# First loads, statistics and skip terms of a gated long-convolution layer in another order

## The reference, cut to what matters

```python
def _layernorm(x, axis=-1, eps=1e-05):
    m = jnp.mean(x, axis=axis, keepdims=True)
    v = jnp.var(x, axis=axis, keepdims=True)
    return (x - m) / jnp.sqrt(v + eps)

def _L0_xattn_ref(k, v, q, ssm_kernel, D, head_dim):      # head_dim 8, 16 heads, L = 256
    kv = jnp.einsum('bhil,bhjl->bijhl', k_, v_)
    kv_f = jnp.fft.rfft(kv, n=fft_size)
    kernel_f = jnp.fft.rfft(ssm_kernel, n=fft_size)
    y = jnp.fft.irfft(kv_f * kernel_f, n=fft_size)[..., :L]
    out = y + kv * D[None, None, None, :, None]           # the skip term
    out = jnp.einsum('bijhl,bhil->bjhl', out, q_)
...
x = x + jnp.tanh(g_xattn[0]) * _L0_xattn_ref(ctx_2048, ctx_2048, _layernorm(x, axis=-1), L0_xattn_ssm_kernel, L0_xattn_D, 8)
```

## Time and profile before

| what | value |
|---|---|
| runs of the kernel | median 958.02 us (956.0 to 959.27, 3 runs) |
| the profiled execution, its own time | 956.07 us |
| its span in the trace | 953.6 us |
| PE busy, share of the span | 910.1 us, 95% |
| DVE, ACT, POOL busy | 605.7, 545.4, 200.7 us |
| mean granted TensorE clock | 0.99 |

### The profile page before, as it was taken

How to read it: one execution, slowest core, us unless ns; L and a number is a source line. 1 busy time by engine, 2 the same in 40 slices (tenths; PEclk the granted TensorE clock), 3 DMA queues, 4 the chain that set the end, 5 groups by cost and what they waited for, 6 DMA issues and landing times.

```text
span 953.6 us, 13986 instructions
## 1 busy us (share of the span) xinstructions
PE 910.1 (95%) x4744; PEld 723.5 (76%) x4744; DVE 605.7 (64%) x1396; ACT 545.4 (57%) x947; POOL 200.7 (21%) x171
## 2 busy tenths in 40 slices
PE   5799889999999999979999988999999999999998
PEld 5799758877788888846666666778788888888886
DVE  6678654555564565478888765656955466556554
ACT  3222043433444335458889675777777777777775
POOL 5899400000000001137777530000000000000000
PEclk9899999999999999999999998999999999999999
DMA  8100120323211351024554305444444344444443
GB/s 299 62 1 1 34 84 17 107 80 114 94 51 35 96 187 58 32 88 156 176 169 156 121 7 166 133 133 132 133 146 150 98 133 133 147 149 136 139 129 109
DMA packets 58101, 104.62 MB, mean 110 GB/s; under 512 B 7312, under 2 KB 13840, under 8 KB 57648
## 3 DMA queue, kind: packets, MB, share of 16 engines
q1 hardware_dynamic: 57312, 103.60, 34.0%
q10 hardware_dynamic: 720, 0.14, 0.1%
HBM read 101.29 MB, written 2.42 MB: 109 GB/s over the span
## 4 chain that ended last, share of the span: by engine, by line
PE 49%; DVE 3%; ACT 2%; issue 1%; DMA 1%; POOL 0%; DVEq 0%; SPq 0%; ACTq 0%; POOLq 0%
PE bank L1111 19%; PE bank L1078 18%; PE bank L1370 3%; PE bank L1381 2%; PE bank L1363 1%; PE bank L1362 1%; PE bank L1358 1%; PE bank L1390 1%; PE bank L534 1%; PE bank L770 1%; DVE X L668 0%; DMA Gf<-gates 0%; DVE shifted_scores L1560 0%; PE bank L752 0%; DVE max L1554 0%
## 5 line engine op out<-in xcount | busy, mean ns | idle before, releaser
L1078 PE MATMUL bank<-xhf,whif 128*128 128x512 f32 x528 | 212.0, 401 | 1.5 <-ACT rf L848 1.5
L1078 PE MATMUL bank<-xlf,whif 128*128 128x512 f32 x528 | 208.2, 394 | 0.0
L1078 PE MATMUL bank<-xhf,wlof 128*128 128x512 f32 x528 | 208.1, 394 | 0.0
L867 ACT ACTIVATE yhif<-yf 128x512 fp32r<-128x512 f32 x200 | 124.1, 622 | 86.6 <-DVE yf L952 82.5
L966 DVE TENSOR_TENSOR yf<-yf,Gf 128x512 f32<-128x512 f32 x125 | 86.5, 692 | 129.3 <-ACT yf L856 122.1
L1111 PE MATMUL bank<-yhif,whif 128*128 128x512 f32 x400 | 159.5, 399 | 7.0 <-DVE ylof L731 6.5
L1111 PE MATMUL bank<-yhif,wlof 128*128 128x512 f32 x400 | 157.9, 395 | 0.0
L1111 PE MATMUL bank<-ylof,whif 128*128 128x512 f32 x400 | 156.9, 392 | 0.0
L731 DVE TENSOR_TENSOR ylof<-yf,yhif 128x512 fp32r<-128x512 f32 x196 | 134.4, 687 | 30.0 <-ACT yhif L867 29.7
L850 ACT ACTIVATE rf<-bank 128x512 f32<-128x512 f32 x136 | 81.0, 596 | 80.7 <-PE bank L1078 80.6
L1078 PEld LDWEIGHTS bank<-xhf,whif 128*128 128x128 f32 x528 | 99.3, 188 | 24.5 <-ACT rf L848 1.9
(11 more groups left out here) (135 smaller groups left out, 1212.2 us busy)
## 6 DMA issues: line engine op xcount, KB each, us to landing
Gf<-gates SPq DMA_DIRECT2D x157, 256.0 KB, 3.7
wrawf<-in_wu SPq DMA_DIRECT2D x68, 256.0 KB, 2.6
k_blocks_sb<-in_k_blk SPq DMA_DIRECT2D x64, 256.0 KB, 4.1
wrawf<-in_wu SPq DMA_DIRECT2D x32, 384.0 KB, 3.2
v_slot<-in_v_rows SPq DMA_DIRECT2D x16, 256.0 KB, 2.7
ctx_windows<-in_ctx_win SPq DMA_DIRECT2D x3, 1024.0 KB, 11.7
toeplitz<-in_kpad SPq DMA_DIRECT2D x4, 512.0 KB, 9.2
X<-in_x SPq DMA_DIRECT2D x4, 512.0 KB, 9.3
```

What stands on the lines that cost most here:

```text
L867: act.activation(yhi[:, K % S, :], y[:, K % S, :], ACT.Copy).then_inc(s_yh, 1)
L1078: last = pe.matmul(o, w_[:, Nu % S, wc], x_[:, c, xs], start=(m == 0), stop=(m == 5))
```

## The change

It moves calls; no instruction is added or taken out.

- SP: the first 512 KB of x (`rows(0)`) are loaded before the first windows and the first kernel table.
- POOL: `pairs(1)` comes behind the first `deviations` and `shifts`.
- ACT: the small loads go in the order `dbc`, `anti`, `ident`; `normed(0)` comes ahead of the second `squares` and of the tanh of the gates.
- PE: the two `turn` calls of group 0 come behind step 1 instead of step 2.
- DVE: the first statistics come ahead of all tables; `table(0)` and `table(1)` follow; `table(2)` comes behind the weighing of step 0 and `table(3)` behind that of step 2. The wait for the tanh moves to group 1.

```diff
@@ SP
+                    rows(0)
                     window_quad(0)
                     kernel_table(0)
-                    rows(0)
                     for hq in range(1, 4):
@@ POOL
                     pairs(0)
-                    pairs(1)
                     pool.wait_ge(s_mh, 1)
                     deviations(pool, "a", 0)
                     shifts(pool, "a", 0)
+                    pairs(1)
                     pairs(2)
@@ ACT
+                    act.dma_start(dbc[:], d_skip.partition_broadcast(P)).then_inc(s_ca, 16)
+                    act.dma_start(anti[:], anti_c).then_inc(s_ca, 16)
                     act.dma_start(ident[:], ident_c).then_inc(s_c, 16)
-                    act.dma_start(anti[:], anti_c).then_inc(s_ca, 16)
-                    act.dma_start(dbc[:], d_skip.partition_broadcast(P)).then_inc(s_ca, 16)
...
                     squares(0)
+                    normed(0)
+                    squares(1)
                     act.wait_ge(s_tl, 32)
                     act.activation(tg[:], graw[:], ACT.Tanh).then_inc(s_tg, 1)
-                    squares(1)
-                    normed(0)
@@ PE
-                            if g == 0 and r == 2:
+                            if g == 0 and r == 1:
                                 for half in range(2):
                                     turn(0, half)
@@ DVE
-                    dve.wait_ge(s_ca, 32)
-                    table(0)
                     input_moments(0)
                     dve.wait_ge(s_st, st.n)
                     variances(dve, "a", 0)
                     negated(dve, "a", 0)
-                    for hq in range(1, 4):
+                    dve.wait_ge(s_ca, 32)
+                    for hq in range(2):
                         table(hq)
-                    dve.wait_ge(s_tg, 1)
                     for g in range(NG):
                         for r in range(8):
                             weigh(g, r // 2, r % 2)
+                            if g == 0 and r in (0, 2):
+                                table(2 + r // 2)
                             if g == 0 and r < 3:
                                 input_moments(r + 1)
...
+                            if g == 1 and r == 0:
+                                dve.wait_ge(s_tg, 1)
```

## The result

| kernel | runs | median us | range |
|---|---|---|---|
| before | 16 | 957.42 | 953.6 to 960.13 |
| changed | 16 | 961.1 | 959.91 to 965.35 |

The ratio of changed to before is 1.005, with a 95% interval of 1.0036 to 1.0063: slower by 3.4 to 6.0 us, 4.8 at the middle; the two medians differ by 3.7. The predicted median was 961.1 us, in a range of 957.5 to 963.5. The profiled execution took 960.74 us, its span is 958.3 us, 4.7 us more than before.

The account below looks back on a forecast made before the run. Stage a was taken as bound by PE's queue from 37.15 us, begun by DVE's statistics chain. Weighing 2.2 us earlier and two tables 1.1 + 4.2 later gave +3.1: median 958.02 + 3.1 = 961.1 us, range 957.5 to 963.5.

Parts of the forecast that it names:

- What bounds the stage: Stage a: from 37.15 us PE's queue, whose end moves one for one with the start of that stretch.
- ident third, and the start of weighing: ACT's queue, PE, DVE: ident lands at 7.3, step 0 starts at 12.5, weighing at 18.7, 2.2 us earlier.
- early-start rival: ident lands by 6.3, weighing starts by 17.7, moments(3) only 1.2 us late, median 959.2 us; chance 0.25.
- signs of being wrong: L405 of 0.34 us beside L255; window group well before 23.6; or weighing starting after 20.9.
- Step 0: PE: starts at 12.5 us instead of 9.03, behind the filler that waits for ident.
- the power: POOL's L139 of 12 columns, for groups 1 to 3: near 35.5 us.
- The hold of table(3): DVE: table(3), due at 27.2, held by POOL's instructions until 31.5; 4.2 us later in the chain.
- L255 holds DVE: Assumed like L246 and L248; the rival without hold: table(3) takes 1.14 us, median 958.0; chance 0.10.
- table(2): DVE: falls at about 20.3 into POOL's pause and is free, adding 1.1 us to the chain.
- hold of the first variances: Group 0's variances, 1.62 us beside pairs(1), no longer stand beside it; costed at 0, covered by steps 0 and 1.
- POOL's pattern: Window group kept landing at 23.64 us; POOL then works without a pause until 31.35.
- clock's price at the turn: PE at granted 0.50 after its gap: same 1.7 us price; rival of a longer clock, 962.8 us, chance 0.15.

Follow-up runs that it names:

- a1: The changed kernel with all four tables back ahead of the first weighing; ratio to before 1.0012.
- c4: c3 with table(3) behind weigh(0), where POOL idles, and the power for groups 2 and 3 two steps later on POOL; ratio to before 0.9951.
- c2: The kernel before with table(3) behind the variances of groups 1 to 3, all else as before; ratio to before 1.0005.
- a2: The changed kernel with ACT's small loads in the old order (ident, anti, dbc); ratio to before 1.0043.
- c5: c4 with filler matmuls in PE's gap ahead of the last four sums; ratio to before 0.9926, median 950.91 us.
- b1: The kernel before with the tables moved alone: table(2) behind weigh(0), table(3) behind weigh(2); ratio to before 1.0031.
- c3: c2 with the statistics of group 1 by themselves, ahead of the first weighing; ratio to before 0.9985.
- a5: The changed kernel with table(3) behind the variances of groups 1 to 3; ratio to before 1.0042, in a second run 1.004.
- a4: The changed kernel with POOL's pairs(5) behind the power and shift of groups 1 to 3; ratio to before 1.0054.

## Why the prediction was right, and where it wasn't

*What bounds the stage.* Right. The `turn` of group 1 was late by 4.51 us, PE behind it was busy throughout, and the span grew by 4.7. a1 and c4 confirm it from both sides. That the end moves one for one with the `turn` holds within about 1 us: c2 lost its 1.0 us at the turn again. The prediction has no term for the clock in the last sums, which cost 1.6 to 3.0 us in seven of the thirteen executions. It was luck that the changed kernel's profiled execution wasn't one of them.

*ident third, and the start of weighing.* This step failed. I took a landing at 7.3, a filler of 5.15 us and a first weighing at 18.7, 2.2 us earlier than before. Measured were 9.15, 6.28 (to 15.43) and 21.48, 0.55 later. The landing varied, 7.0 to 9.5 us over six executions with that order; from the filler's start to step 0 it was 5.2 to 6.6 us over all the executions but a2's, where step 0 waited for the first table, with the granted clock rising sooner or later in it. I had one value for each and no spread. The landing that I had taken it from, `dbc` third in the old order, varied as well: 5.7 us from its issue in the kernel before and 5.5 in c5, but 7.1 to 7.5 in b1, c2, c3 and c4. With 7.4, the forecast would have been near the 9.15 that came. The early-start rival fell with it: `ident` landed by 6.3 us in none of the seven executions in which it was third.

For that rival I had read the Trainium skill, "DMA: Bandwidth & Descriptors", section "Queues, rings and completion order", as if taking the queue rows in turn kept ACT's small loads from being late. The runs contradict that reading and not the rule itself: with the same loads on SP's queue `ident` took 2.9 us from issue to landing in the first place of ACT's queue (a2) and 5.3 to 7.7 in the third, so what made it late stood in its own queue.

With it came true one of the signs of being wrong that I had named, weighing that starts after 20.9. Step 0 (15.43 for 12.5), the power (36.87 for 35.5) and the `turn` were each later than forecast.

*The hold of table(3).* Right in mechanism, off in place and size. I had it due at 27.2, with 4.2 us to the next instruction; it came at 29.89 and took 2.91, of which 1.86 are the hold. Since a later start meets fewer of POOL's instructions, the two errors took each other back in part: +0.55 + 1.05 + 2.91 = 4.51 against the predicted -2.2 + 1.1 + 4.2 = 3.1. That L255 holds DVE was assumed; b1 showed it.

*The rest.* table(2) was free (1.13 us). The hold of the first variances, which I had removed with pairs(1), came back in pairs(0): from 9.27 they took 1.99 us in the changed kernel. It cost nothing, as predicted, since the turn of group 0 waited for step 1. The window group landed at 24.45 instead of 23.64, so POOL's pattern came 0.8 us later than I had held fixed; with x first the pairs of group 1 started between 23.14 (a2) and 24.45 over seven executions. The clock's price at the turn was nearly the same, 3.69 us of slow PE against 3.40, although the gap was 8.55 instead of 4.85:

```profile
41.67:45.36 3.69, 3.69 (x13) 3.50 (x14) 0.00 (x0) 1.36 (x3) 3.69 (x4) 0.50 0.00 0
```

The exact agreement of the median, 961.1, is partly luck: the trace's sum was 4.5, not 3.1, the forecast of +3.1 lies just below the measured 3.4 to 6.0 us, and the runs of the kernel before centred 0.6 us lower than the three first ones. I had given slower and same 0.47 each; at 0.5%, over the bound of 0.3% that I had drawn, it is slower.

## What to carry to other kernels

A short instruction on DVE with two SBUF inputs isn't short beside POOL's products and sums (L246, L248, L255): count it as the time to the end of the POOL instruction that runs, and look for a place where POOL idles, as c4 did (1.1 us instead of 4.4), or where it does something that doesn't hold DVE, as its power in a5 (1.14 us). Before work is moved between the steps of a chain, ask which result the next engine really needs first; splitting the statistics, so that group 1 didn't wait for groups 2 and 3, gave at most a little with a held table behind it (c3, 1.4 us), and 4.7 us with the table moved to POOL's pause as well (c4). The table's move without the split wasn't run. And of a load in a queue behind others, take a spread from several executions, not one landing.

## What the runs showed of the hardware that I had not expected

The clock of the last sums. In seven of thirteen profiled executions the 32 transposes behind 3.1 us of idle PE ran wholly or partly at a granted 0.50, 5.3 to 6.7 us instead of 3.71, with the same step and the same 3.1 us gap right ahead of them as in the six that ran at 1.00. In three of the seven (a1, a4 and the second run of a5) the clock fell only about 1 us after they had started. The landing of one 64 KB load, third in its queue, was 7.0 or above 9.1 us with x first, with nothing in between over six executions.

The power. POOL's L139, with two inputs like its products and sums, didn't hold the tables: four instructions of DVE ran beside it in 1.13 or 1.14 us in a5, its second run and c2, as long as beside an idle POOL. The power itself took 2.39 us there and 2.28 or 2.29 alone.
